# One comparison of two broadcast tensors for a step's one-hots: the first stage of a graph-network kernel

## The chip, the cores and the metric

The kernel runs on one core of one Trainium2 chip. The metric is the device time of one execution in microseconds (us). The engines are PE (TensorE), DVE (VectorE), ACT (ScalarE), POOL (GpSimd) and SP (SyncE, which only issues transfers here). They run at once and meet at semaphores.

## What is computed

Four graph layers follow each other on 3125 nodes of 32 features and 100000 edges (`src`, `dst`). Each is a layer norm, a ReLU, the layer, and a residual sum:

```
h = max(layernorm(x), 0);  x = x + L0(h)     # agg = segment_sum(edge_attr, src); MLP of [h, agg]; batch norm
h = max(layernorm(x), 0);  x = x + L1(h)     # messages from h[src], a radial net of edge_weight, rel_vec; summed by dst
h = max(layernorm(x), 0);  x = x + L2(h)     # 3 rounds out = clip(0.9 * A_w out + 0.1 * h, 0, 1)
h = max(layernorm(x), 0);  x = x + L3(h)     # 3 rounds of normalised adjacency product, relu, batch norm
```

What matters here is the first line's `segment_sum(edge_attr, src)`: for every node, the sum of the 32 attributes of the edges that leave it.

## The kernel before

Edges stand in 784 chunks of 128, one edge for each partition, and a **step** is 4 chunks: 196 steps in the first stage, 196 in the second. The sum over edges is a matrix product. A node number is split as a = node / 640 (0 to 4) and b = node mod 640. For each chunk k of a step there is a **one-hot** `onehot0[:, q, k, :]` of 640 columns (1 where the column is the edge's b), and `prod0[:, q, k]` of 5 x 64 columns, which holds the edge's attributes (in a high and a low part) at the place of its a and zeros elsewhere. PE multiplies the five 128-column parts of the one-hot with `prod0` and adds to five PSUM banks (`scatter0`, L914, 5 matmuls a chunk, 20 a step). q is the step's buffer, one of two.

One-hots are made by two engines. ACT makes chunk 0 of each step, and chunk 1 too in every fourth step, as relu(1 - (column - b)^2) (`onehots`, L668 and L673; `by_act` says which). DVE makes the other three, or two in every fourth step, at L1311: the columns' numbers `iota_b` compared with the edge's b, a column of `b_src`, one instruction for each chunk. b_src is fp32, iota_b is fp32, and the one-hot is written as fp32r.

Beside this, the stage finds edges with equal (src, dst) keys, since the later layers need the adjacency matrix. For each **group** of 4 chunks: ACT compares keys (L643, L648), DVE masks (`mark_group`, L1249, signals `s_tri`), PE counts (`merge_open`, L885 to L893, then three dependent `merge_hop`, L899, each fed by a one-column DVE instruction `live_entries`, L1297), and DVE writes the rows and values to be added (`group_entries`, L1257 to L1262, signals `s_idx`). There are half as many groups as steps, so that 392 of the 784 chunks have their entries by the end of the first stage.

POOL adds these entries to the matrix in device memory: `add(c)`, L585, one indirect transfer for each chunk, whose row numbers it reads from `sc_idx`. It first zeroes the matrix with 41 large transfers and waits for all of them; then come adds 0 to 391 in a fixed order, **and only then**, on the same queue, `gather(0)` (L593), with which the second stage begins: DVE's first instruction of that stage (L1433) waits for it. The gather also waits for `s_feat`, the store of the node table, which SP issues when DVE has set `s_table` (L1426) after the MLP between the stages.

The order on each engine is the order of the code. DVE's step in the first stage: mark the group (even steps); wait until the step two before is summed; at every fourth step split the attributes (L1308); one-hots (L1311); at every fourth step the low part (L1316); `live_entries`; `prod0` (L1320, `s_prod[0]`); `live_entries`; in odd steps the entries. `s_ohv` tells PE that DVE's one-hots of the step are there; PE also waits for `s_prod[0]` before the step's first matmul, and `prod0` stands behind the one-hots on DVE. SP loads the attributes of four steps (`load_attr`) as their buffer comes free. Four steps are one pass of the hardware loops, here called a **cycle**; there are 49.

Of the kernel before, what the change touches and what calls it, by code (L numbers as in the profile page):

```python
# [16 lines left out]
ALU = mybir.AluOpType  # L17
# [8 lines left out]
P = 128  # L26
# [8 lines left out]
PARTS = 5  # L35
# [50 lines left out]
def ds(start, size):  # L86
    if isinstance(start, int):
        return slice(start, start + size)
    return bass.ds(start, size)


def gnn_program(nc, x_in, src_in, dst_in, srcT_in, dstT_in, ea3_in, ea32_in, ew_in, ewT_in,
                w1T_in, b1_in, gamma_in, beta_in, w2T_in, b2_in, l1w1_in, l1b1_in, l1w2_in, l1b2_in,
                gam3_in, bet3_in, out):
    with ExitStack() as ctx:
        def sb(name, shape, dt=F32):
            return ctx.enter_context(nc.sbuf_tensor(name, shape, dt))

        def sem(name):
            return ctx.enter_context(nc.semaphore(name))  # L100
# [11 lines left out]
        iota_b = sb("iota_b", [P, PARTS * P])  # L112
# [25 lines left out]
        def edge(*dims, dt=F32, parts=P):  # L138

            n = 1  # L140
            for d in dims:
                n *= d
            words = n // 2 if dt == BF16 else n
            lo = placed[0]
            placed[0] += words
            assert placed[0] <= KEPT * NP - 8 * HI * 2 * FEAT
            v = kept_all[0:parts, lo:lo + words]
            if dt != F32:
                v = v.bitcast(dt)
            if len(dims) == 1:  # L150
                return v
            names = ["d%d" % i for i in range(len(dims))]
            return v.rearrange("p (%s) -> p %s" % (" ".join(names), " ".join(names)), **dict(zip(names, dims)))
# [5 lines left out]
        b_src = edge(CH)  # L159
# [67 lines left out]
        def placed_at(name, shape, end):  # L227

            n = 4
            for d in shape[1:]:  # L230
                n *= d
            return nc.alloc_sbuf_tensor_at(name, shape, F32R, offset=end - n)

        prod0 = placed_at("prod0", [P, 2, 4, HI, 2 * FEAT], kept_end)
        onehot0 = placed_at("onehot0", [P, 2, 4, PARTS * P], big_end - 4 * NP)
# [65 lines left out]
        s_ohv = sem("p0_onehot_dve_ready")  # L301
# [68 lines left out]
        def first(s, n=2):  # L370

            return isinstance(s, int) and s < n
# [10 lines left out]
        def by_act(k4):  # L383

            return (0, 1) if k4 == 3 else (0,)
# [757 lines left out]
        def _(dve):  # L1143
# [14 lines left out]
            V = nc.vector  # L1158
# [85 lines left out]
            def mark_group(g, slot):  # L1244

                dve.wait_ge(s_same, 2 * g + 2)
                if not first(g):
                    dve.wait_ge(s_ded, 2 * g - 2)
                V.tensor_tensor(same_tri[:, slot, :, :], same[:, slot, 1:11:3, :],  # L1249
                                earlier[:, :].unsqueeze(1).broadcast_to([P, 4, P]), ALU.mult).then_inc(s_tri, 2)  # L1250

            def group_entries(g, slot):

                if not first(g, 1):
                    dve.wait_ge(s_idx, 2 * g)
                m = ps[:, 2 + slot, 0:28].rearrange("p (j v) -> p j v", j=4)
                V.tensor_reduce(sc_val[:, ds(2 * g, 2), :, :].rearrange("p d j v -> p (d j) v"),  # L1257
                                m[:, :, 1:7].rearrange("p j (v i) -> p j v i", i=3), AX, ALU.add)
                V.scalar_tensor_tensor(out=offs[:, :], in0=m[:, :, 0], scalar=0.0, in1=to_spare[:, ds(4 * g, 4)],
                                       op0=ALU.is_gt, op1=ALU.mult).then_inc(s_offs, 2)  # L1260
                dve.wait_ge(s_offs, 2 * g + 2)
                V.tensor_tensor(sc_idx[:, ds(4 * g, 4)], offs[:, :], key[:, ds(4 * g, 4)], ALU.add).then_inc(s_idx, 2)  # L1262
# [32 lines left out]
            def live_entries(slot, j):  # L1295

                V.tensor_scalar(live[:, slot, j:j + 1], ps[:, 2 + slot, 7 * j:7 * j + 1], 0.0, None,  # L1297
                                ALU.is_equal).then_inc(s_live, 1)

            def phase0(s, k4, u):  # L1300
                q, g, slot = k4 % 2, u * 2 + k4 // 2, k4 // 2
                if q == 0:
                    mark_group(g, slot)
                if not first(s):
                    dve.wait_ge(s_sum[0], 4 * (s - 1))
                if k4 == 0:
                    dve.wait_ge(s_attr, 64 * u + 64)
                    V.tensor_scalar(rows0[:, :, 0, :].bitcast(I32), attr[:, :, :].bitcast(I32), -4096, None,  # L1308
                                    ALU.bitwise_and).then_inc(s_hi, 1)
                for k in range(len(by_act(k4)), 4):  # L1310
                    ins = V.tensor_scalar(onehot0[:, q, k, :], iota_b[:, :], b_src[:, ds(4 * s + k, 1)], None,  # L1311
                                          ALU.is_equal)
                ins.then_inc(s_ohv, 1)
                if k4 == 0:
                    dve.wait_ge(s_hi, u + 1)
                    V.tensor_tensor(rows0[:, :, 1, :], attr[:, :, :], rows0[:, :, 0, :], ALU.subtract).then_inc(s_rows, 1)  # L1316
                dve.wait_ge(s_hop, 3 * g + 1 + 2 * q)
                live_entries(slot, 2 * q)
                dve.wait_ge(s_rows, u + 1)
                V.tensor_tensor(prod0[:, q, :, :, :], high0[:, ds(4 * s, 4), :].unsqueeze(3)  # L1320
                                .broadcast_to([P, 4, HI, 2 * FEAT]),
                                rows0[:, 4 * k4:4 * k4 + 4, :, :].rearrange("p k t f -> p k (t f)").unsqueeze(2)
                                .broadcast_to([P, 4, HI, 2 * FEAT]), ALU.mult).then_inc(s_prod[0], 4)
                if q:
                    dve.wait_ge(s_ded, 2 * g + 2)
                else:
                    dve.wait_ge(s_hop, 3 * g + 2)
                live_entries(slot, 2 * q + 1)
                if q:
                    group_entries(g, slot)  # L1330

            dve.wait_ge(s_keysd, 64)
            for s in range(4):
                phase0(s, s, 0)
            with dve.Fori(1, SETUP_AT) as u:
                for k4 in range(4):
                    phase0(u * 4 + k4, k4, u)


            dve.wait_ge(s_in["x"], 16)  # L1340
            center()
            phase0(4 * SETUP_AT, 0, SETUP_AT)
            split_nodes(dst_i, a_dst, b_dst, False).then_inc(s_edge, 1)
            phase0(4 * SETUP_AT + 1, 1, SETUP_AT)
# [30 lines left out]
            for part in range(PARTS):  # L1375
                ins = V.tensor_reduce(cat[:, part:NA:PARTS, 32:64], ps[:, SUM0[part], 0:HI * 2 * FEAT]
                                      .rearrange("p (a t f) -> p a f t", a=HI, t=2), AX, ALU.add)
# [6 lines left out]
            for n, (c0, w) in enumerate(NCOL):  # L1384
                dve.wait_ge(s_act0, n + 1)
                ins = V.bn_stats(bnst[:, n, :], actT[:, c0:min(c0 + w, NODES)])
# [27 lines left out]
            for a0, a1, bank in ((0, A_LO, 4), (A_LO, NA, 5)):  # L1414
                ins = V.tensor_tensor(x[:, a0:a1, :], x[:, a0:a1, :],
                                      ps[:, bank, 0:(a1 - a0) * 32].rearrange("p (a f) -> p a f", f=32), ALU.add)
# [64 lines left out]
            for part in range(PARTS):  # L1481
                acc = part_sums(part, MSG).rearrange("p (a m) -> p a m", m=MSG)
                mine = slice(part, NA, PARTS)
                V.tensor_tensor(x[:, mine, :], x[:, mine, :], acc[:, :, 0:32], ALU.add)
                ins = V.tensor_copy(deg[:, mine, :], acc[:, :, 32:34])
# [12 lines left out]
            def part(a0, a1, bank):  # L1498
                return ps[:, bank, 0:(a1 - a0) * FEAT].rearrange("p (a f) -> p a f", f=FEAT)
# [24 lines left out]
            for r in range(3):  # L1524
# [5 lines left out]
                for a0, a1, bank in turned:  # L1530
                    ins = V.tensor_tensor(sq[:, a0:a1, :], part(a0, a1, bank),  # L1531
                                          dinv[:, 0, a0:a1].unsqueeze(2).broadcast_to([P, a1 - a0, FEAT]), ALU.mult)
# [63 lines left out]
            for r in range(3, 6):  # L1596
                for b in range(BANKS):
                    mine = slice(b * BANK_D, (b + 1) * BANK_D)
# [9 lines left out]
                    if b:  # L1608
                        ins = V.tensor_tensor(fsum[:, 0, :], fsum[:, 0, :], fsum[:, 5, :], ALU.add)
# [68 lines left out]
```

## Time and profile before

| | |
|---|---|
| median of 3 runs | 3467.55 us (3462.26 to 3476.69) |
| the profiled execution, span | 3465.3 us |
| PE, DVE, ACT, POOL busy, of the span | 86%, 79%, 66%, 62% |
| zeroing of the matrix lands, first add starts | 211.9 us |
| first stage on PE and DVE ends | about 977 us |
| node table ready (L1426) | 1023.3 us |
| last of the 392 adds of this part, first gather | 1055.7, 1057.6 us |
| second stage starts on DVE (L1433) | 1063.9 us |

All times are microseconds from the span's start. In a row of a timeline the columns are start, duration (for "x3", from the first start to the last end), engine, line, operation, output and inputs with their shapes, and in brackets how long the engine had been idle and who released it. A duration covers an instruction from start to end; instructions of one engine overlap by nearly 0.1 us, so the distance from one start to the next is what one costs a busy engine.

### The profile page before, as it was taken

How to read it: one execution, taken by the hardware profiler on the slowest of the kernel's cores; microseconds unless marked ns; L12 is line 12 of the kernel's file. 1: busy time of each engine (PE TensorE's matmuls, PEld its weight loads, DVE VectorE, ACT ScalarE, POOL GpSimd, SP SyncE). 2: the span in 40 equal slices, each digit the busy share in tenths (PEclk: the TensorE clock that was granted, in tenths of full speed). 3: DMA queues.
4: the chain of work that ended last, by engine and by line, in shares of the span. 5: the costliest groups of instructions: out<-in, count | busy, mean ns of one | idle time of the engine just before them, and what ended most of it. 6: DMA issues, size and time to landing. Idle time of an engine off the chain costs nothing. (4 is left out here: it accounts for less than half of the span.)

```text
span 3465.3 us, 69301 instructions
## 1 busy us (share of the span) xinstructions
PE 2974.6 (86%) x19703; PEld 2370.4 (68%) x19703; DVE 2742.9 (79%) x6018; ACT 2280.7 (66%) x3192; POOL 2141.3 (62%) x1629
## 2 busy tenths in 40 slices
PE   3888788988856999999999999999999976657657
PEld 3677677777745888888888888888888851113257
DVE  6678988888856999999999999999999973441065
ACT  3678688888836888888888888888888842220000
POOL 4048888888877777777777777777777730000000
PEclk9899899999977999999999999999999997798778
DMA  9943222222222333333333333333333359998940
GB/s 400 419 154 38 12 15 15 15 16 16 15 25 41 53 53 52 50 53 51 50 53 51 50 53 51 51 53 52 50 53 52 50 187 426 426 391 342 373 172 6
DMA packets 265695, 388.67 MB, mean 112 GB/s; under 512 B 149903, under 2 KB 200838, under 8 KB 259254
## 3 DMA queue, kind: packets, MB, share of 16 engines
q0 software_dynamic: 149184, 120.78, 20.7%
q1 hardware_dynamic: 100034, 195.42, 16.6%
q10 hardware_dynamic: 16416, 71.74, 5.1%
q8 instruction: 28, 0.46, 0.1%
q14 instruction: 33, 0.27, 0.0%
HBM read 260.01 MB, written 127.78 MB: 112 GB/s over the span
## 5 line engine op out<-in xcount | busy, mean ns | idle before, releaser
L585 POOL DMA_INDIRECT both<-kept x782 | 1333.0, 1705 | 439.8 <-issue 194.6
L923 PEld LDWEIGHTS ps<-prod,big 128*128 128x128 f32 x7840 | 1133.9, 190 | 137.7 <-DVE prod L1290 133.0
L923 PE MATMUL ps<-prod,big 128*128 128x170 f32 x7840 | 1183.2, 310 | 22.5 <-DVE prod L1290 17.4
L593 POOL DMA_INDIRECT kept<-feat_dram,kept x782 | 760.8, 973 | 243.2 <-issue 233.1
L668 ACT ACTIVATE big<-iota_b,kept 128x640 f32<-128x640 f32 x1029 | 779.0, 815 | 13.6
L914 PE MATMUL ps<-prod,onehot 128*128 128x320 f32 x3920 | 684.5, 325 | 81.2 <-DVE prod L1320 79.6
L914 PEld LDWEIGHTS ps<-prod,onehot 128*128 128x128 f32 x3920 | 597.7, 194 | 112.9 <-DVE prod L1320 84.5
L673 ACT ACTIVATE big<-big 128x2560 f32<-128x2560 f32 x196 | 458.0, 2337 | 277.2 <-PE ps L923 277.1
L988 PE MATMUL ps<-w2mix,kept 65*128 65x384 f32 x1568 | 559.3, 500 | 21.7 <-ACT kept L720 20.4
L1462 DVE TENSOR_REDUCE kept<-kept 128x80 f32<-128x1280 f32 x392 | 561.4, 1471 | 0.0
L988 PEld LDWEIGHTS ps<-w2mix,kept 65*128 65x128 f32 x1568 | 284.2, 191 | 179.7 <-issue 25.5
L1452 DVE TENSOR_TENSOR kept<-ps,kept 128x384 f32<-128x384 f32 x784 | 395.3, 544 | 0.0
L616 POOL DMA_INDIRECT prod<-both,row_idx x8 | 7.8, 977 | 526.2 <-DVE row_idx L1570 512.4
L1320 DVE TENSOR_TENSOR prod<-kept 128x1280 fp32r<-128x1280 f32 x196 | 291.9, 1489 | 4.3
L1311 DVE TENSOR_SCALAR onehot<-iota_b,kept 128x640 fp32r<-128x640 f32 x539 | 291.4, 593 | 0.0
L673 ACT ACTIVATE onehot<-big 128x640 fp32r<-128x640 f32 x196 | 171.1, 873 | 182.4 <-PE ps L914 173.7
L1129 PE MATMUL ps<-big,zring 128*32 128x512 f32 (+3 forms) x400 | 183.5, 615 | 118.6 <-DMA big<-both 106.8
L1448 DVE TENSOR_TENSOR kept<-ps,kept 128x512 f32<-128x512 f32 x392 | 266.1, 679 | 0.0
L643 ACT ACTIVATE kept<-ps,kept 128x128 f32<-128x128 f32 (+2 forms) x588 | 223.3, 477 | 0.0
L1129 PEld LDWEIGHTS ps<-big,zring 128*32 128x32 f32 x400 | 45.3, 124 | 256.8 <-issue 242.3
L1520 DVE TENSOR_REDUCE row_max<-big 128x1 f32<-128x1600 f32 x50 | 91.0, 1819 | 160.0 <-DMA adj_c<-kept 107.6
L765 ACT ACTIVATE kept<-big 128x1600 f32<-128x1600 f32 x50 | 82.2, 1648 | 187.0 <-issue 83.2
(235 smaller groups left out, 3028.9 us busy)
## 6 DMA issues: line engine op xcount, KB each, us to landing
both<-big POOLq DMA_DIRECT2D x40, 1910.0 KB, 91.2
big<-both SPq DMA_DIRECT2D x24, 1600.0 KB, 11.8
big<-both SPq DMA_DIRECT2D x24, 1528.0 KB, 13.2
kept<-keys_dram SPq DMA_DIRECT2D x196, 128.0 KB, 3.0
kept<-in_wT SPq DMA_DIRECT2D x196, 128.0 KB
adj_c<-kept ACTq DMA_DIRECT2D x42, 400.0 KB, 31.6
kept<-adj_c SPq DMA_DIRECT2D x9, 1600.0 KB, 22.4
adj_w<-kept ACTq DMA_DIRECT2D x16, 800.0 KB, 33.6
```

The source lines that it names most:

```text
L585: pool.indirect_dma_start(both, bass.IndirectOffsetOnAxis(ap=sc_idx[:, c:c + 1], axis=0), sc_val[:, c // 2, c % 2, :], None, compute_op=AL ...
L593: pool.indirect_dma_start(gath[:, s % 2, k, :], None, feat_dram, bass.IndirectOffsetOnAxis(ap=src_i[:, 4 * s + k:4 * s + k + 1], axis=0)). ...
L668: act.activation(dist[:, k, :], iota_b[:, :], ACT.Square, scale=-1.0, bias=bcol[:, ds(4 * s + k, 1)]).then_inc(s_dist[n], 4 // len(ks))
L673: act.activation(to[:, q, 0:len(ks), :], dist[:, 0:len(ks), :], ACT.Relu, scale=-1.0, bias=1.0).then_inc(s_oh[n], 1)
L914: mm = pe.matmul(ps[:, SUM0[part], 0:HI * 2 * FEAT], onehot0[:, q, k, part * P:(part + 1) * P], prod0[:, q, k, :, :].rearrange("p a m -> p ...
L923: mm = pe.matmul(part_sums(part, MSG), onehot[:, q, k, part * P:(part + 1) * P], prod[:, q, k, 0:HI * MSG], start=False, stop=False, skip_ ...
L988: mm = pe.matmul(ps[:, 4 + k, 0:384], hidT[:, q, k * P:(k + 1) * P], w2mix[:, :], start=True, stop=True)
L1311: ins = V.tensor_scalar(onehot0[:, q, k, :], iota_b[:, :], b_src[:, ds(4 * s + k, 1)], None, ALU.is_equal)
L1320: V.tensor_tensor(prod0[:, q, :, :, :], high0[:, ds(4 * s, 4), :].unsqueeze(3) .broadcast_to([P, 4, HI, 2 * FEAT]), rows0[:, 4 * k4:4 * k4 ...
L1448: V.tensor_tensor(T[:, :, 0:256].rearrange("p k (o x) -> p k o x", o=16), ps[:, 4 + 2 * g:6 + 2 * g, 0:256].rearrange("p k (o x) -> p k o ...
L1452: ins = V.tensor_tensor(T[:, k, 256:640].rearrange("p (u i x) -> p u i x", u=8, i=3), ps[:, 4 + 2 * g + k, 256:384].rearrange("p (u x) -> ...
L1462: V.tensor_reduce(res[:, q, 2 * g:2 * g + 2, 0:40], terms[:, g, :, :].rearrange("p k (o x) -> p k o x", x=16), AX, ALU.add).then_inc(s_red, 1)
```

## The change

DVE's two or three comparisons of a step (tensor with a scalar column, 128 x 640 each) become one comparison of two tensors, 128 x 1920 or 128 x 1280. Its first input reads `iota_b` anew for each chunk, its second reads each of the step's `b_src` values 640 times. ACT's part, the semaphores and all waits stay; `s_ohv` is still signalled once a step.

```
-                for k in range(len(by_act(k4)), 4):
-                    ins = V.tensor_scalar(onehot0[:, q, k, :], iota_b[:, :], b_src[:, ds(4 * s + k, 1)], None,
-                                          ALU.is_equal)
-                ins.then_inc(s_ohv, 1)
+                mine = len(by_act(k4))
+                V.tensor_tensor(onehot0[:, q, mine:4, :], iota_b[:, :].unsqueeze(1).broadcast_to([P, 4 - mine, PARTS * P]),
+                                b_src[:, ds(4 * s + mine, 4 - mine)].unsqueeze(2)
+                                .broadcast_to([P, 4 - mine, PARTS * P]), ALU.is_equal).then_inc(s_ohv, 1)
```

On DVE, at the first two steps of a cycle (`kept` is the large buffer in which `b_src`, the attributes and the masks lie):

```order
 L1249 TENSOR_TENSOR kept<-kept,earlier 128x512
 L1308 TENSOR_SCALAR kept<-kept 128x16x32
-L1311 TENSOR_SCALAR onehot_50<-iota_b,kept 128x640 x3
+L1311 TENSOR_TENSOR onehot_50<-iota_b,kept 128x1920
 L1316 TENSOR_TENSOR kept<-kept 128x16x32
 L1297 TENSOR_SCALAR kept<-ps 128x1
 L1320 TENSOR_TENSOR prod_49<-kept 128x1280
 L1297 TENSOR_SCALAR kept<-ps 128x1
-L1311 TENSOR_SCALAR onehot_50<-iota_b,kept 128x640 x3
+L1311 TENSOR_TENSOR onehot_50<-iota_b,kept 128x1920
```

Nothing changes its place; three rows become one. PE's rows are the same as before.

## Rows read from the trace of the kernel before

**Rows 1.** Busy time by stretch (start:end length, each engine's busy us and instructions, clock, DMA).
```profile
215.00:977.00 762.00, 665.89 (x4731) 579.00 (x4732) 653.17 (x1391) 604.47 (x946) 634.67 (x354) 0.98 0.25 17
977.00:1057.40 80.40, 29.33 (x104) 19.26 (x102) 30.33 (x52) 20.58 (x31) 61.75 (x37) 0.58 0.30 31
```

**Rows 2.** Waits, 977 to 1064 us, then 215 to 977 us (us, times, longest).
```profile
DVE kept L1433 <- DMA kept<-feat_dram,kept: 40.6, 1, 40.6
...
PE ps L914 <- DVE prod L1320: 66.4, 85, 1.4
DVE kept L1297 <- PE ps L899: 63.4, 140, 0.9
```

**Rows 3.** Timeline between the stages: POOL's last add and first gather; DVE; the table's store.
```profile
1055.73 1.54 POOL L585 DMA_INDIRECT both<-kept  x1 [0.30 <-issue]
1057.58 1.02 POOL L593 DMA_INDIRECT kept<-feat_dram,kept  x1 [0.30 <-issue]
...
1063.94 0.28 DVE L1433 TENSOR_TENSOR kept<-kept 128x96 f32<-128x96 f32 x1 [40.63 <-DMA kept<-feat_dram,kept]
...
feat_dram<-big SPq DMA_DIRECT2D x1, 1200.0 KB, 6.4
```

**Rows 4.** Groups by line: POOL's adds in the two stretches, split at 977.02 us.
```profile
L585 POOL DMA_INDIRECT both<-kept x355 | 637.5, 1796 | 297.6 <-DMA both<-big 171.0 <-issue 115.3 <-DMA both<-kept 9.3
...
L585 POOL DMA_INDIRECT both<-kept x37 | 61.8, 1669 | 19.5 <-issue 11.3 <-DMA both<-kept 8.2
```

**Rows 5.** Timeline of DVE through one cycle, from its L1308 to the next.
```profile
601.77 0.42 DVE L1308 TENSOR_SCALAR kept<-kept 128x512 int32<-128x512 int32 x1
602.11 1.78 DVE L1311 TENSOR_SCALAR onehot<-iota_b,kept 128x640 fp32r<-128x640 f32 x3
603.81 0.67 DVE L1316 TENSOR_TENSOR kept<-kept 128x512 f32<-128x512 f32 x1
...
606.12 1.76 DVE L1311 TENSOR_SCALAR onehot<-iota_b,kept 128x640 fp32r<-128x640 f32 x3
607.99 0.16 DVE L1297 TENSOR_SCALAR kept<-ps 128x1 bf16<-128x1 f32 x1
608.13 1.49 DVE L1320 TENSOR_TENSOR prod<-kept 128x1280 fp32r<-128x1280 f32 x1
609.99 0.16 DVE L1297 TENSOR_SCALAR kept<-ps 128x1 bf16<-128x1 f32 x1 [0.37 <-PE ps L899]
...
611.26 1.53 DVE L1311 TENSOR_SCALAR onehot<-iota_b,kept 128x640 fp32r<-128x640 f32 x3
612.71 0.15 DVE L1297 TENSOR_SCALAR kept<-ps 128x1 bf16<-128x1 f32 x1
...
614.27 1.20 DVE L1311 TENSOR_SCALAR onehot<-iota_b,kept 128x640 fp32r<-128x640 f32 x2
616.12 0.16 DVE L1297 TENSOR_SCALAR kept<-ps 128x1 bf16<-128x1 f32 x1 [0.65 <-PE ps L899]
...
619.65 0.42 DVE L1308 TENSOR_SCALAR kept<-kept 128x512 int32<-128x512 int32 x1
```

**Rows 6.** Groups of DVE, 215 to 977 us; then its two-broadcast comparison L1370 by itself.
```profile
L1311 DVE TENSOR_SCALAR onehot<-iota_b,kept 128x640 fp32r<-128x640 f32 x455 | 250.0, 601 | 0.0
L1320 DVE TENSOR_TENSOR prod<-kept 128x1280 fp32r<-128x1280 f32 x166 | 247.2, 1489 | 3.6
...
977.80 4.24 DVE L1370 TENSOR_TENSOR high<-iota_a,kept 128x3920 bf16<-128x3920 f32 x1 [2.65 <-PE ps L914]
```

**Rows 7.** Timeline: adds of POOL that met a DVE instruction, and that instruction.
```profile
978.87 4.58 POOL L585 DMA_INDIRECT both<-kept  x1 [0.30 <-issue]
...
715.16 2.66 POOL L585 DMA_INDIRECT both<-kept  x1 [0.30 <-issue]
718.12 1.54 POOL L585 DMA_INDIRECT both<-kept  x1 [0.30 <-issue]
...
714.91 1.49 DVE L1320 TENSOR_TENSOR prod<-kept 128x1280 fp32r<-128x1280 f32 x1
...
718.04 1.53 DVE L1311 TENSOR_SCALAR onehot<-iota_b,kept 128x640 fp32r<-128x640 f32 x3
```

**Rows 8.** Timeline of DVE while the matrix is being zeroed, and POOL's first add.
```profile
181.67 1.47 DVE L1311 TENSOR_SCALAR onehot<-iota_b,kept 128x640 fp32r<-128x640 f32 x3
183.05 0.68 DVE L1316 TENSOR_TENSOR kept<-kept 128x512 f32<-128x512 f32 x1
...
202.62 0.43 DVE L1308 TENSOR_SCALAR kept<-kept 128x512 int32<-128x512 int32 x1 [2.38 <-DMA kept<-in_ea]
...
211.90 1.68 POOL L585 DMA_INDIRECT both<-kept  x1 [170.98 <-DMA both<-big]
```

## The prediction, made before the changed kernel ran

> **What bounds the kernel now.** I read the busy time by stretches first. Until 977 us PE and DVE are both near full, 666 and 653 of 762 us [rows 1]; then come 80 us in which PE and DVE are each busy for 30 us and POOL for 62. The view of waits says why: DVE stands 40.6 us before its first instruction of the second stage, for a gather [rows 2]. The timeline shows the gather at 1057.58, right behind the last add of POOL's queue (1055.73 + 1.54 + 0.30), and DVE 6.4 us behind it, at 1063.94 [rows 3]. The table that the gather reads was ordered stored at 1023.3 and its store took 6.4 us, so from 1030 on the gather waited for nothing but its turn. So **two chains race to the second stage**: (A) DVE and PE through 49 cycles, then the MLP, table, store and gather, ready at 1023.3 + 6.4 + 6.4 = 1036; (B) POOL's 392 adds from 211.9 on, then the gather, 1064. B wins by 28 us. Everything later hangs on this start and holds no L1311, so what the change does to the time is what it does to 1063.9.
>
> **DVE's price of the change.** A comparison of tensor and column takes 601 ns in the mean [rows 6]; three that nothing disturbs take 183.05 - 181.67 = 1.38 us from first start to the next instruction [rows 8], three that POOL disturbs up to 603.81 - 602.11 = 1.70 [rows 5]. For the new form there are two kinds of row: 1280 elements in 1.49 us (L1320, with broadcast inputs too) and 3920 in 4.24 us, L1370, which is a comparison of the same kind with the same two broadcasts [rows 6]. The slope is 2.75 us / 2640 = 1.04 ns an element, against 0.46 us for 640, 0.72 ns, in the old form. So 1920 elements take 1.49 + 640 x 1.04 = 2.16 us, 2.07 to the next start, and the pair 1.49 (1.40). A cycle has three of the one and one of the other: 3 x 2.07 + 1.40 = 7.6 us, against 11 x (0.601 - 0.09) = 5.6: 2.0 us more of DVE's time.
>
> Fewer instructions is what the Trainium skill asks for (VectorE: DVE Perf Modes, section Rules for kernel authors: minimise the number of chained operations). By that alone the change would gain. The rows put the saving of two starts at about 0.25 us and the slower stream at 0.9, so the rows decide against it.
>
> **What of it reaches the end of the stage.** I walk DVE through the cycle of [rows 5], whose length is 619.65 - 601.77 = 17.88 us; from 405.5 to 958.7 us, 31 cycles have the mean 17.84.
> - Step 1: 1.70 becomes 2.07, and all behind it, PE's matmuls included, comes 0.37 later.
> - Step 2: the one-hots end before PE's hop comes (DVE reaches L1297 at 607.99, where it had to wait for PE a moment); `prod0` ends 0.52 later, but live 3 waits for PE anyway (0.37 idle, at 609.99) and PE is itself 0.37 late. Added: nothing.
> - Step 3: the group took 612.71 - 611.26 = 1.45 and DVE did not wait behind it: plus 0.62.
> - Step 4: the pair ends at 615.4 and DVE waits 0.65 for PE. 0.3 longer goes into that wait. Nothing.
>
> Sum: 0.37 + 0.62 = **1.0 us a cycle**, period 18.87. PE's waits for `prod0` grow with it (now 66 us in all [rows 2]). For 41 cycles from 215 us on this is 41. In the 8 cycles before, where DVE waits for the attributes (2.38 us at 202.62 [rows 8]), the order of their load hangs on `prod0` of step 3, which comes 2 x (2.07 - 1.38) = 1.4 later: 11. **The stage ends 53 us later, at about 1030**, chain A at 1089. Bounds: nothing if DVE's waits for PE (63 us [rows 2]) swallowed all, 49 x 2.0 = 98 if none was swallowed. I take 53 because the walk names each wait.
>
> **POOL's price.** An add takes 1.54 us when alone, and 355 of them had 1796 ns in the mean [rows 4]. What stretches them is DVE. At 978.87 an add lasted 4.58 us: L1370, from 977.80, ended at 982.04, and the add ended 1.41 us after that. At 715.16 one lasted 2.66: L1320 ended at 716.40, the add 1.42 after [rows 7]. So an add that begins while a two-tensor instruction runs is held to its end, then needs 1.41, and the pause to the next is 0.30. Against the short comparisons it often loses nothing: at 718.12 an add began 0.08 after the first of three and took 1.54. So the short ones let POOL in between, and the new one of 2.16 us does not. The Trainium skill has this as a rule (SBUF — State Buffer, section Who interferes with whom: a DVE instruction with two SBUF inputs contends with a GpSimd instruction that reads SBUF); the trace agrees by the 4.58 us. It also counts a column comparison in its two-port mode as a full blocker, and then little would change; 1.54 at 718.12 speaks against.
>
> Now the new cycle of 18.87 us, with 0 at L1308. The two-tensor instructions stand at 0.34 to 2.50, 2.41 to 3.09, 3.24 to 4.73, 4.72 to 6.88, 6.88 to 8.37, 9.86 to 12.02, 12.00 to 13.49, 13.49 to 14.98 and 15.47 to 16.96. I put an add at 2.2: held to 2.50, ends 3.9; next 4.3, held to 4.73, ends 6.1; next 6.5, held to 6.88, ends 8.3; next 8.65, free, ends 10.2; next 10.55, held to 12.02, ends 13.4; next 13.8, held to 14.98, ends 16.4; next 16.75, held to 16.96, ends 18.4; next 18.7, ends in the next cycle at 1.5, and 1.85 again falls in the first one. It closes: **8 adds a cycle, 2.36 us an add**, against (977 - 211.9) / 355 = 2.155 now. Other phases close at 7 or near 8.3, 2.27 to 2.70.
>
> **The sum.** POOL has done (1030 - 211.9) / 2.36 = 347 adds when the stage ends. 45 are left, at the rate of the stretch behind it, 80.4 / 37 = 2.18 [rows 4]: 98 us. The gather starts at 1128 in place of 1057.6: **plus 70 us**. Against the profiled span that is 3465.3 + 70 = 3535.7; the median of the runs is 2.25 above the span, so 3467.55 + 70 = **3538 us**. All comes from B: A, at 1089 against B's 1134, is now 45 behind.
>
> **Rivals.**
> 1. *POOL is not held more than now* (2.155 an add; only the old rate of collisions). Then 380 adds are done at 1030, 12 left, the gather could go at 1057 as now, and chain A decides: 1089 against 1064, +25: 3493. For it: the new instruction writes through one stream and its second input is 3 numbers; against it: L1370 has the same inputs. The Trainium skill has a sentence that would give this (same page and section): `tensor_tensor` was not seen to stall transfers of POOL's queue, taken there as needing only the write side. The 4.58 us again speaks against. Chance 0.12.
> 2. *POOL is freed and DVE swallows the rest*: the side of a gain. If the column comparisons were what stretches adds, adds would go at 1.54 + 0.31 = 1.85 and B would be done with the stage; A would decide, at 1036 plus what the stage grows. It is a gain if the stage grows by less than 28 us, that is if DVE's added 2.0 a cycle sinks into its 63 us of waits for PE and the attribute loads. With 15 of growth: 1051, -13: 3455. Against: steps 1 and 3 have no wait behind the one-hots. Chance 0.06, half of it within 0.5%.
> 3. *POOL locks in at 7 adds a cycle*, 2.70: 303 done at 1030, 89 left, 194 us, gather at 1224, +166: 3634. It needs the phase at which two long instructions in a row each hold an add in full in both halves of the cycle. Chance 0.07.
> 4. *The stage grows by 98, not by 53*: the end at 1075, 366 adds at 2.36, 26 left, 57 us: 1132, +74; A at 1134 against 1138 for B. The sum hardly moves, since a longer stage also gives POOL more time. That is why I trust the middle: B depends on the rate of adds, and only at (2.36 - 2.18) / 2.36 = 8% on the stage's length.
>
> That the change does not do what it says I exclude: the built program has one instruction of 1920 elements where three stood.
>
> **How the numbers follow.** Forecast 0.75, around +70. Its own range comes from the rate: at 2.27, 360 done, 32 left, 70 us, 1100, +43; at 2.50, 327 done, 65 left, 142 us, 1172, +114. So 3510 to 3582. To hold 8 in 10 I go down to rival 1 and leave out 3: 3490 to 3585. About 0.5%, 17 us, is what a measurement here can tell from no change. Slower by more: 0.75 + 0.12 + 0.07 and a little less for a rival 1 that falls short: 0.92. Within: 0.05. Faster: 0.03.
>
> **What would show it.** L1311 128x1920 at 2.16 and 128x1280 at 1.49 us; L1308 to L1308 18.9 us; the stage's end near 1030; adds in the stage with a mean of 2.0 us (2.36 with their pauses) in place of 1.80, and many of 2.5 to 3.5; DVE idle before L1433 for some 58 us in place of 40.6; L593 first at 1128; the second stage and all behind it as long as before. It is wrong if the first gather comes when the table is stored, not behind an add (rival 1 or 2), if adds of 1.54 us stand across an L1311, or if the cycle is 19.9 long or under 18.3.

## The result, and the profile after

The changed kernel takes 3534.66 us in the median of 4 runs (3527.84 to 3535.88), the one before 3464.91 (3445.91 to 3476.69): the ratio on record is 1.0213, with a 95% interval of 1.0192 to 1.0234. (The recorded ratios, here and below, are not the quotients of the two medians, 1.0201 here, and differ from them by up to 0.0012.) The forecast was 3538 and slower. The number came out; the way to it did not wholly, as the profile shows. Its span is 3532.0 us.

First the two prices. Groups of DVE between 215 and 1069 us, and of POOL up to the end of the stage (line, output and inputs, count, busy us, mean ns, idle before); they answer to [rows 6] and [rows 4]:

```profile
L1311 DVE TENSOR_TENSOR onehot<-iota_b,kept 128x1920 fp32r<-128x1920 f32 x125 | 268.8, 2150 | 0.0
L1320 DVE TENSOR_TENSOR prod<-kept 128x1280 fp32r<-128x1280 f32 x168 | 250.0, 1488 | 3.4
L1311 DVE TENSOR_TENSOR onehot<-iota_b,kept 128x1280 fp32r<-128x1280 f32 x42 | 62.2, 1481 | 0.0
...
L585 POOL DMA_INDIRECT both<-kept x371 | 735.7, 1983 | 292.5 <-DVE kept L1262 171.2 <-issue 118.1 <-DMA both<-kept 3.2
```

Both are as forecast: 2150 ns for 1920 elements (2.16), 1481 for 1280 (1.49), and an add has grown from 1796 to 1983 ns. The timeline of POOL with the DVE instruction that it met, as in [rows 7]:

```profile
704.28 1.54 POOL L585 DMA_INDIRECT both<-kept  x1 [0.30 <-issue]
706.13 3.00 POOL L585 DMA_INDIRECT both<-kept  x1 [0.30 <-issue]
...
705.56 2.15 DVE L1311 TENSOR_TENSOR onehot<-iota_b,kept 128x1920 fp32r<-128x1920 f32 x1
```

The new comparison ends at 707.71, the add that came into it 1.42 us later. So it is throughout: of the 371 adds of the stage 166 began inside an L1311, and 165 of them ended 1.41 to 1.44 us after it; the last began as it ended and took 1.54.

Then the place between the stages, which answers to [rows 3]: POOL's last add and first gather, DVE's last instruction before and first behind:

```profile
1112.11 1.78 POOL L585 DMA_INDIRECT both<-kept  x1 [0.37 <-issue]
1120.79 1.03 POOL L593 DMA_INDIRECT kept<-feat_dram,kept  x1 [6.90 <-DMA feat_dram<-big]
...
1113.75 0.42 DVE L1426 COPY big<-h 128x400 f32<-128x400 f32 x1
1128.14 0.26 DVE L1433 TENSOR_TENSOR kept<-kept 128x96 f32<-128x96 f32 x1 [13.97 <-DMA kept<-feat_dram,kept]
```

The second stage starts at 1128.1 instead of 1063.9, 64.2 later, of the span's 66.8. But the gather does not stand right behind the last add. That ended at 1113.89; the gather waited 6.9 us for the table's store. **Chain A decides, by 6.6 us.** This is one of the prediction's own signs of being wrong: the gather came when the table was stored, and DVE stood idle before L1433 for 14.0 us, not 58. The stage on DVE and PE ends not at 1030 but at 1069.2 (start of L1370): 91.4 us later, not 53.

Where do 38 us more come from? The starts of L1308 give the cycles. Of the 31 cycles before the last L1308, 15 last 18.9 us, which is the forecast's 18.87, and the other 16 last 20.4. No other length occurs there. Busy time over the stretch of the 31 cycles, over 100 us of it, and over a piece of the last cycle, which follows them (columns as in [rows 1]; the third number from the end is the granted clock, a share of 2.4 GHz). The first row is of the kernel before, from the same time to its last L1308:

```profile
438.30:958.70 520.40, 465.40 (x3327) 403.57 (x3325) 443.65 (x963) 427.83 (x673) 434.36 (x243) 1.00 0.25 16
...
438.30:1047.60 609.30, 519.72 (x3534) 448.90 (x3534) 523.34 (x808) 450.54 (x708) 524.41 (x264) 0.95 0.22 14
700.00:800.00 100.00, 84.86 (x583) 73.26 (x583) 86.88 (x135) 74.28 (x117) 86.20 (x44) 0.97 0.23 15
...
1054.50:1057.10 2.60, 2.60 (x10) 2.40 (x10) 1.59 (x2) 0.00 (x0) 2.29 (x2) 0.50 0.21 1
```

In the kernel before, the clock stood at full from 410 to 980 us. Here it falls to half, 1.2 GHz, for 3.4 us in every cycle of 20.4 us, and in none of 18.9. The timeline of PE and DVE through such a piece, in the last cycle, which begins at 1047.57:

```profile
1050.79 0.18 PE L899 MATMUL ps<-kept 128*128 128x1 bf16 x1 [0.41 <-DVE kept L1297]
1052.45 1.94 PE L914 MATMUL ps<-prod,onehot 128*128 128x320 f32 x10 [1.49 <-DVE prod L1320]
1054.20 0.23 PE L899 MATMUL ps<-kept 128*128 128x1 bf16 x1
1054.29 3.01 PE L914 MATMUL ps<-prod,onehot 128*128 128x320 f32 x10
1057.11 0.21 PE L899 MATMUL ps<-kept 128*128 128x1 bf16 x1
...
1054.60 1.50 DVE L1320 TENSOR_TENSOR prod<-kept 128x1280 fp32r<-128x1280 f32 x1
1057.37 0.16 DVE L1297 TENSOR_SCALAR kept<-ps 128x1 bf16<-128x1 f32 x1 [1.28 <-PE ps L899]
```

PE stood 0.41 and 1.49 us at the head of the cycle, then worked 1.9 us; then ten matmuls took 3.01 us in place of 1.7, and DVE, which waits for the hop behind them, lost 1.28 where the kernel before had lost 0.37 [rows 5] and a short cycle of the changed one (at 704.30) loses 0.27. That is what makes a cycle long.

What did PE do differently before the clock fell? In the kernel before it has one long wait in a cycle, 1.40 us at the head, and the clock stays up. In the changed kernel it has three, in short and long cycles alike: 0.42 and 1.39 at the head and 0.88 before step 3. The rows are the head's wait before, the two of `prod0` in a short cycle after, and all waits of this kind from 215 us to the stage's end (us, times, longest), 96.9 us where it had been 66.4 [rows 2]:

```profile
606.19 1.73 PE L914 MATMUL ps<-prod,onehot 128*128 128x320 f32 x10 [1.40 <-DVE prod L1320]
...
700.49 1.74 PE L914 MATMUL ps<-prod,onehot 128*128 128x320 f32 x10 [1.39 <-DVE prod L1320]
709.24 1.76 PE L914 MATMUL ps<-prod,onehot 128*128 128x320 f32 x10 [0.88 <-DVE prod L1320]
...
PE ps L914 <- DVE prod L1320: 96.9, 87, 1.5
```

The rest of the program, from L1433 to the end, takes 2403.9 us, before 2401.3: nothing was lost or won there.

### The profile page after: what moved, and what is told of

It is laid out like the page before. It is cut to its first block and busy times, and to the rows that moved or that the text cites. A ratio compares the mean times of both kernels' runs of the same rounds, so it can differ in the third digit from the quotient of the medians.

```text
span 3532.0 us, 68628 instructions
## 1 busy us (share of the span) xinstructions
PE 3012.2 (85%) x19702; PEld 2401.0 (68%) x19703; DVE 2831.8 (80%) x5675; ACT 2280.5 (65%) x3192; POOL 2214.0 (63%) x1629
## 5 line engine op out<-in xcount | busy, mean ns | idle before, releaser
L585 POOL DMA_INDIRECT both<-kept x782 | 1405.8, 1798 | 424.0 <-issue 191.6
L914 PE MATMUL ps<-prod,onehot 128*128 128x320 f32 x3920 | 715.7, 335 | 112.9 <-DVE prod L1320 112.9
L914 PEld LDWEIGHTS ps<-prod,onehot 128*128 128x128 f32 x3920 | 625.3, 202 | 149.8 <-DVE prod L1320 115.4
L1311 DVE TENSOR_TENSOR onehot<-iota_b,kept 128x1920 fp32r<-128x1920 f32 x196 | 388.6, 1983 | 0.0
L1320 DVE TENSOR_TENSOR prod<-kept 128x1280 fp32r<-128x1280 f32 x196 | 291.7, 1488 | 4.0
L1290 DVE TENSOR_TENSOR prod<-high,kept 128x680 f32<-128x680 f32 (+1 forms) x196 | 170.2, 868 | 43.8 <-DVE kept L1471 43.4
```

What stands on the lines that cost most here:

```text
L585: pool.indirect_dma_start(both, bass.IndirectOffsetOnAxis(ap=sc_idx[:, c:c + 1], axis=0), sc_val[:, c // 2, c % 2, :], None, compute_op=AL ...
L914: mm = pe.matmul(ps[:, SUM0[part], 0:HI * 2 * FEAT], onehot0[:, q, k, part * P:(part + 1) * P], prod0[:, q, k, :, :].rearrange("p a m -> p ...
L1311: V.tensor_tensor(onehot0[:, q, mine:4, :], iota_b[:, :].unsqueeze(1).broadcast_to([P, 4 - mine, PARTS * P]), b_src[:, ds(4 * s + mine, 4 ...
```

## The experiments

All positions below are from profiles; "stage end" is the start of L1370, "start" that of DVE's first instruction of the second stage. From the start on, the rest took 2399 to 2404 us in every run but the last two, so a shift of the start is a shift of the total. Experiments 2 to 9 ran once each; positions of one kernel can differ by some us between runs (the stage end of the kernel before is 977.8 and, where only later adds are missing, 981.0). So a difference of a few us between two of them means nothing by itself; what released the gather, and how long the cycles are, can be read from one run. Where an edit added lines, line numbers behind it are shifted.

| kernel | stage end | usual lengths of the last 31 cycles (one number: their mean) | adds: us from one to the next, mean us of one | start | what the gather waited for |
|---|---|---|---|---|---|
| before | 977.8 | 17.8 | 2.15, 1.795 | 1063.9 | last add |
| changed | 1069.2 | 18.9, 20.4 | 2.31, 1.983 | 1128.1 | table's store |
| 1, PE kept busy | 1034.4 | 18.9 | 2.41, 2.073 | 1148.6 | last add |
| 2, before, 40 adds less | 981.0 | 17.8 | 2.14, 1.783 | 1039.7 | table's store |
| 3, changed, 40 adds less | 1070.9 | 18.9, 20.4 | 2.34, 1.993 | 1128.9 | table's store |
| 4, comparisons cut | 1103.7 | 19.2, 20.7 | 2.29, 1.890 | 1162.6 | table's store |
| 5, before, no adds | 968.9 | 17.6 | none | 1027.5 | table's store |
| 6, changed, no adds | 1071.6 | 18.9, 20.4 | none | 1130.7 | table's store |
| 7, steps 2 and 4 | 978.7 | 17.8 | 2.23, 1.898 | 1087.8 | last add |
| 8, steps 1 and 3 | 1080.4 | 18.9, 20.4 | 2.31, 1.971 | 1139.1 | table's store |
| 9, as 1, 40 adds less | 1032.5 | 18.9 | 2.41, 2.069 | 1091.6 | table's store |

### 1. PE kept busy

```
                 g, slot = u * 2 + (k4 + 1) // 2, (k4 + 1) // 2 % 2
+                for _ in range((5, 0, 3, 0)[k4]): pe.matmul(ps[:, SUM0[0], :], zero_bf[:, 0:P], zero_bf[:, :], start=False, stop=False, skip_group_check=True)
                 scatter0(s, k4, 0)
```

> The changed kernel with eight extra matmuls a cycle on PE (zeros times zeros, 512 columns, added to a bank that they leave as it is): five before the first matmul of step 1, three before step 3, where PE waits for prod0. In the changed kernel the cycles last either 18.88 or 20.37 us, and in each long one the granted clock stands at half for 3.4 us. Theory: the long cycles are PE at half clock after its longer waits; with PE kept busy all cycles last 18.9, the stage ends at about 1025 in place of 1069, and then POOL's adds decide (349 done by then, 43 left at 2.2 us), gather near 1119, second stage near 1125: total about 3 us under the changed kernel, 3530. Rival, that the long cycles come from DVE or from POOL's adds: they stay at 20.4, the stage ends at 1069 or later. Rival, that POOL's adds do not decide even then: start near 1083, total near 3487.

Busy time and the clock over the same stretches; then the timeline of POOL's last add and first gather and of PE at the head of a cycle; then the wait of DVE (its line has moved by one):

```profile
438.30:1047.60 609.30, 555.54 (x3811) 457.09 (x3873) 541.76 (x832) 456.61 (x715) 523.63 (x253) 0.99 0.23 14
700.00:800.00 100.00, 92.86 (x644) 76.96 (x654) 89.26 (x140) 76.99 (x123) 85.82 (x41) 1.00 0.22 15
```

```profile
1140.37 1.54 POOL L585 DMA_INDIRECT both<-kept  x1 [0.43 <-issue]
1142.22 1.02 POOL L593 DMA_INDIRECT kept<-feat_dram,kept  x1 [0.30 <-issue]
...
715.86 1.02 PE L933 MATMUL ps<-zero_bf 128*128 128x512 bf16 x4 [0.49 <-issue]
716.76 1.74 PE L914 MATMUL ps<-prod,onehot 128*128 128x320 f32 x10
```

```profile
DVE kept L1434 <- DMA kept<-feat_dram,kept: 68.4, 1, 68.4
```

The long cycles are gone (30 of the last 31 last 18.9, the first 20.5 behind a half-clock stretch that ends at 434 us), and the clock stays full from 434 to 1038 us. PE's wait at the head is 0.49 in place of 1.39. The mean of the 31 cycles is 18.94 us, and the stage ends at 1034.4, 56.6 us later than before; the forecast had 53. So the walk through DVE's cycle was right at full clock, and the other 34.8 us are PE at half clock. A count agrees: the changed kernel has 16 falls of the clock in its last 31 cycles and 9 between 212 and 385 us, and 25 times 1.5 us is 37. Yet the kernel is **no faster than the changed one**: 3551.32 us (3545.01 to 3553.65) where the kernel before had 3476.53 on the same chip, ratio 1.0208 (1.0186 to 1.0230), against 1.0213 for the changed kernel. In the profiles its start is even 20.5 us later. With DVE quicker through the stage, POOL had 341 adds done at its end and 51 left; those took 108 us, and DVE stood 68.4 us for the gather. This is the race as it was forecast (347 done, 45 left, gather at 1128), with the gather 14 us later still: the add took 2.41 us, not 2.36. My expectation for this run, 349 adds by 1025 us (2.33 each) and a total of 3530, was too low. So an end of the stage 35 us earlier moved the bound back to POOL.

### 2 and 3. Forty adds less

```
-            for c in range(CH // 2):
+            for c in range(CH // 2 - 40):
                 add(c)
```

(with the counts of later waits lowered by 20 for each of the two semaphores)

> The kernel before, with the last 40 adds of the first stage left out (their entries are missing from the matrix). Theory that POOL's queue sets the start of the second stage: the gather goes as soon as the table is stored, near 1030, the second stage starts near 1036 in place of 1064, total 28 us less. Rival, that something else holds the gather: no change.

> The changed kernel with the same 40 adds left out. Theory that in it DVE and PE's chain decides (its trace shows the gather waiting 6.9 us for the table's store): start at 1128 as in the changed kernel, total the same within 5 us. Rival, as the prediction had it, that POOL's queue decides by far: the start moves up by some 45 us, total 3490.

POOL's first gather, of the kernel before and of the changed one, each without 40 adds:

```profile
1032.53 1.02 POOL L593 DMA_INDIRECT kept<-feat_dram,kept  x1 [66.52 <-DMA feat_dram<-big]
```

```profile
1122.29 1.02 POOL L593 DMA_INDIRECT kept<-feat_dram,kept  x1 [88.08 <-DMA feat_dram<-big]
```

In the kernel before the start comes at 1039.7, 24.2 us earlier (its stage ended 3 us late in this run). Its bound was POOL's queue. In the changed one nothing moves, 1128.9 against 1128.1. Its bound is DVE and PE. So the change swapped the bound, and of chain A's growth, 91.4, the 24 to 27 us were free by which POOL had been behind.

### 4. One comparison for each chunk, still of two tensors

In place of the changed kernel's one instruction:

```
+                for k in range(len(by_act(k4)), 4):
+                    ins = V.tensor_tensor(onehot0[:, q, k, :], iota_b[:, :],
+                                          b_src[:, ds(4 * s + k, 1)].broadcast_to([P, PARTS * P]), ALU.is_equal)
+                ins.then_inc(s_ohv, 1)
```

> The changed kernel with the comparison of two tensors cut into one for each chunk (128 x 640, both inputs tensors; two or three instructions again). Each takes (4.24 - 1.49) / 2640 x 640 us less than a 1280 one, 0.82, three take 2.2 to the next instruction against 2.07: cycles about 0.3 longer than those of the changed kernel, 19.2 and 20.7. Theory, that an add is held to the end of the one instruction that it meets: adds in the stage are shorter, mean 1.85 in place of 1.98 us. Rival, that every two-tensor instruction holds POOL in turn: mean 1.98 or more.

```profile
704.61 1.55 DVE L1311 TENSOR_TENSOR onehot<-iota_b,kept 128x640 fp32r<-128x640 f32 x2
```

Two of them take 1.55 us, a single one 0.81. Cycles are 19.2 and 20.7 as expected, but 25 of the last 31 are long ones, where the changed kernel has 16, so that the stage ends at 1103.7. Adds have a mean of 1.890 us (expected 1.85), 0.09 less than in the changed kernel with even more two-tensor time on DVE: what holds an add is the one instruction that it meets, and its length counts. The total, 3568, is 33 us worse than the changed kernel's, as its start is 34.5 us later: chain A lost it.

### 5 and 6. No adds at all

(as in 2 and 3, with 392 for 40 and 196 for 20)

> The kernel before with all 392 adds of the first stage left out (half of the matrix's entries are missing), so that POOL does nothing while DVE and PE work. It shows DVE and PE's chain alone. Theory: the only thing that adds do to DVE is to stretch some column comparisons (1.70 us for three in place of 1.38): cycles 17.5 in place of 17.85, stage's end near 963 in place of 978, second stage 62 us behind that, near 1024.

> The changed kernel with all 392 adds of the first stage left out. Theory, that a two-tensor instruction is not stretched by an add and that the long cycles are PE's clock: cycles 18.9 and 20.4 as in the changed kernel, end of the stage at 1065 to 1070, second stage near 1125, so that the change costs about 100 us where POOL plays no part. Rival, that the long cycles come from adds: all cycles 18.9, end near 1035.

```profile
704.74 1.47 DVE L1311 TENSOR_SCALAR onehot<-iota_b,kept 128x640 fp32r<-128x640 f32 x3
```

With POOL silent, three column comparisons take 1.47 us each time in place of 1.78 at the cycle's head [rows 5], a cycle of the kernel before lasts 17.57 us, and the stage ends 8.9 us earlier (15 expected). The changed kernel does not care: 18.9 and 20.4 again, 1071.6. Chain A alone costs the change 102.7 us, where 100 were expected. The rival that adds make the long cycles is out: with no add there are 18 of them in the last 31.

### 7 and 8. The change in half of the steps

```
-                mine = len(by_act(k4))
+                if k4 in (1, 3):
+                    mine = len(by_act(k4))
...
+                for k in range(len(by_act(k4)), 4 if k4 not in (1, 3) else 0):
```

(and with (0, 2) in the eighth)

> The change in the second and fourth step of each cycle alone. In the walk of the prediction both groups end before PE's hop is done, so they cost DVE and PE nothing: cycles 17.9 to 18.0, no half clock, stage's end within 5 us of 978. POOL's adds are held longer by these two: 2.2 to 2.3 us an add in place of 2.15, and since POOL's queue decides in the kernel before, the second stage starts 10 to 35 us later than 1064. Rival: all groups cost alike, then the stage's end is at 1020 or later.

> The change in the first and third step of each cycle alone, whose groups stand on the chain through prod0 to PE. Theory: all of the growth is here: cycles 18.9 and 20.4, half clock as in the changed kernel, stage's end 1055 to 1072, second stage 60 us behind it, total 3515 to 3535. Rival, all groups cost alike: stage's end near 1025.

DVE in the second step of a cycle of the seventh; L1312 is the new comparison, L1325 prod0:

```profile
715.39 2.15 DVE L1312 TENSOR_TENSOR onehot<-iota_b,kept 128x1920 fp32r<-128x1920 f32 x1
717.46 0.15 DVE L1297 TENSOR_SCALAR kept<-ps 128x1 bf16<-128x1 f32 x1
717.53 1.48 DVE L1325 TENSOR_TENSOR prod<-kept 128x1280 fp32r<-128x1280 f32 x1
719.27 0.16 DVE L1297 TENSOR_SCALAR kept<-ps 128x1 bf16<-128x1 f32 x1 [0.26 <-PE ps L899]
...
1081.43 1.02 POOL L593 DMA_INDIRECT kept<-feat_dram,kept  x1 [0.30 <-issue]
```

Steps 2 and 4 cost DVE and PE nothing: stage end 978.7 against 977.8, DVE still waits for PE behind the second (0.26), and the clock stays full from 413 to 983 us. But the start is 23.8 us later, by POOL's queue alone: an add takes 2.23 us. Steps 1 and 3 bring all of chain A's growth, even more than the whole change: 1080.4, with 22 long cycles in the last 31 where the changed kernel has 16. I had expected at most 1072, and a total of at most 3535, where 3543 was measured. What makes a cycle long in one kernel more often than in the other is not explained.

### 9. PE kept busy and forty adds less

The edits of the first and the third experiment together.

> The changed kernel with the extra matmuls of the first experiment and with the last 51 - 11 = 40 adds of the first stage left out. Theory: the extra matmuls keep PE's clock up (stage's end 1034), and what then held the gather was POOL's queue (1142), so that with fewer adds the gather goes at 1142 - 40 x 2.1 = 1058 or, if the table comes later, behind its store at 1087: second stage near 1094, total near 3497. That is the changed kernel with both of its second-hand costs (clock and queue) taken away: 53 to 56 us of the 91 left over. Rival, that the matmuls themselves or something else held the start: 1125 or later.

```profile
1084.69 1.03 POOL L593 DMA_INDIRECT kept<-feat_dram,kept  x1 [26.42 <-DMA feat_dram<-big]
```

The start is at 1091.6, total 3494.06. With both second-hand costs taken away the start is 27.7 us behind that of the kernel before with all its adds (1063.9), and 51.9 behind that of the kernel before with the same adds left out (1039.7). The second is the like comparison: the 53 of the walk.

### 10 and 11. Could the kernel before gain its 24 us?

The queue is the bound before the gather, so I moved the gather ahead of the last 16 adds, and spread these over the second stage.

```
-            for c in range(CH // 2):
+            for c in range(CH // 2 - 16):
                 add(c)
             pool.wait_ge(s_feat, 16)
             gather(0, range(4))
...
-                if s >= BEHIND:
-                    for c in range(2 * (STEPS + s - BEHIND), min(2 * (STEPS + s - BEHIND) + 2, USED)):
-                        add(c)
+                while c < min(max(CH // 2, 2 * (STEPS + s - BEHIND) + 2) - max(0, 16 - 2 * (s + 1) if s < 2 else 16 - 4 - s // 8), USED):
+                    add(c); c += 1
```

(in the eleventh `2 * (s // 16)` in place of `s // 8`)

> The kernel before, with the first gather of the second stage moved ahead of the last 16 adds of the first on POOL's queue; those adds follow in the second stage, 2 in each of the first two steps, then one more than usual every eighth step. Theory: POOL's queue holds the second stage by 24 to 28 us, so it starts at 1040 in place of 1064, and as POOL's pauses in the second stage take up 16 adds of 1.9 us, nearly all of it stays: 3440 to 3447, 0.6 to 0.8% faster. Rival, that POOL has no room in the second stage: the gathers come later step by step and the second stage is longer by up to 16 x 1.9 = 30 us, total as before.

```profile
1506.08 1.60 POOL L593 DMA_INDIRECT kept<-feat_dram,kept  x1 [0.30 <-issue]
1507.98 1.61 POOL L585 DMA_INDIRECT both<-kept  x1 [0.30 <-issue]
1512.44 1.58 POOL L585 DMA_INDIRECT both<-kept  x1 [2.85 <-issue]
1514.32 1.01 POOL L593 DMA_INDIRECT kept<-feat_dram,kept  x1 [0.30 <-issue]
```

The start came at 1036.8, 27.1 us earlier, and the rest took 2553.8 us, 152 longer: 3592.77 us (3592.17 to 3602.28), ratio 1.0390 (1.0371 to 1.0409). My edit had a flaw: each even chunk's add waits until the odd one before it has landed, and with a single add put in, that odd one stands right in front, so that the even one waits 2.85 us, as in the third row. The expected 3440 to 3447 was missed by far.

> As the tenth experiment, but the 12 adds that are left after the first two steps follow in pairs, 2 more than usual in every sixteenth step, so that an even chunk's add never comes right behind the odd one whose landing it has to wait for (in the tenth, where single adds were put in, adds came in the wrong pairs and waited 2.9 us of each step, and the second stage took 152 us longer). Theory: the wrong pairs were all of it; the start stays at 1037. In the second stage of the kernel before POOL's queue has no pause beyond the 0.3 us between instructions, so 16 adds of 1.9 us and 6 waits of 2.9 for landings cost up to 47 us there, as far as POOL and not PE decides: total 3440 to 3480, likely within 0.5% of before. Rival, that POOL has room in the second stage: 3438, 0.7% faster.

In pairs the start is at 1045.9 (1037 expected; in this run the stage ended at 987.0, 9 us late) and the rest 2443.4: 18 us won ahead and 42 lost behind. 3488.95 us (3486.67 to 3494.76) against 3471.03 on that chip, ratio 1.0053 (1.0034 to 1.0072): just above the expected 3440 to 3480, and a small loss. The rival with room in the second stage is out. From 1200 to 2700 us of the kernel before, POOL is busy for 1194 us and its pauses of 0.3 us make another 303, all but 3 of the 1500: moving its work there is no gain, and I have no version that beats the kernel before.

## Why the prediction was right, and where it was not

**What bounds the kernel now:** right. Experiment 2 took POOL's 40 adds away and the start moved by 24.2 us; 28 was forecast.

**DVE's price:** right to 0.01 us, from L1370 and L1320 (2.15 and 1.48 measured, 2.16 and 1.49 forecast).

**The walk through the cycle:** right as far as it went. 18.9 us for 18.87; steps 2 and 4 nothing, 1 and 3 all (experiments 7 and 8); by the end of the first 8 cycles DVE was 9.8 us late for 11; stage end 1034 with PE's clock kept up, for 1030. (In step 2 `prod0` comes 0.57 later by the rows, not 0.52; nothing hangs on it.)

**The step that failed: "for 41 cycles this is 41".** It took every cycle as alike and PE's speed as given, though the walk itself had said that PE's waits for `prod0` grow. They grew from 66 to 97 us in the stage, and from 212 us to the stage's end PE stood at half clock for 116 us, where it had been 24, the more in pieces of 3.4 us. That term, 34.8 us (1069.2 against 1034.4), was missing. It was named nowhere, not even among the rivals; rival 4 had the size (98) but another cause.

**POOL's price:** right in kind and within 2% in size. For 2.36 it was 2.31 us an add in the changed kernel, whose cycles are longer than those of the walk, and 2.41 in experiment 1, which has the walk's cycles. The mechanism, held to the end of the instruction that an add meets and 1.41 more, shows in the row at 706.13 and in experiment 4. Rival 1, that POOL is not held more, is out by 1983 ns against 1796 and by experiment 7, where chain A did not grow and the start moved by 23.8 us. What it expected of the gather, to go when the table is stored, came true for another reason.

**"All comes from B":** wrong. A decides (experiment 3). The total came out within 3.4 us because the two chains lean on each other: time that A loses is time in which POOL goes on adding. The forecast had the gather at 1128 by B and at 1083 by A; it could have gone at 1114.2 by B and went at 1120.8 by A. That the number was right is thus half luck. With the missing 34.8 us put in, the prediction's own prices give a stage end of 1065, 361 adds done and 31 left, B's gather at 1132 and A's at 1118: 4 us more in the total and still the wrong chain ahead, since adds at 2.36 for 2.31 are 18 us too dear over the stage. And the fall of the clock taken away (experiment 1) gave no faster kernel, since B then stands at 1142.2.

**Rival 2**, a gain, needed waits that swallow DVE's 2 us a cycle. Steps 2 and 4 swallowed theirs; 1 and 3 did not. **Rival 3**, 7 adds a cycle (2.70 us each), did not occur in any run; the highest was 2.41.

## What to carry to other kernels

Merging VectorE instructions pays only while the merged form loses less in its stream than the starts that it saves: here three fp32 comparisons with a column took 1.38 us, one comparison of two tensors with the same elements 2.07. Ask of a longer instruction also whom it locks out: here each add that POOL began inside it waited for its end (165 of 166). And where an engine's waits grow, price that engine at its lower clock too, and keep both chains of a race in the sum to the end, with what a loss of one gives to the other: taking one cost away (experiment 1) gave no faster kernel.

## What the runs showed of the hardware

- An indirect transfer of POOL that meets a two-tensor DVE instruction is held to its end and then needs 1.41 us: 4.58 us behind L1370, 3.00 behind a comparison of 2.15. In the other direction, three column comparisons take 1.47 us with POOL silent and up to 1.78 with it [rows 5]; a two-tensor one of 1920 elements keeps its 2.15 in both (experiment 6).
- The granted clock of PE fell from 1.0 to 0.5 for 3.4 us at a time in cycles in which PE had waited 0.42 and 1.39 us at the head and 0.88 before step 3, though none of these waits was longer than 1.5 us and PE was busy for 85 of the 100 us from 700 on. In the kernel before, a wait of 1.40 at the head of every cycle left it at 1.0. Five bf16 matmuls on zeros at the head and three before step 3 kept it at 1.0; which of the waits it takes was not tried one by one. The short cycles of the changed kernel have the same waits, and in the later part two short ones follow two long ones; what chooses them stays open.
- What one such fall costs is 1.5 us of a cycle, read from 20.4 against 18.9.
